# First attention fed tile group by tile group, causal quarter left constant, router chain spread between products

## Chip, cores and metric

The kernel is one Bass program on one core of a Trainium2 chip. The metric is device time in microseconds (us) of one execution. The engines are TensorE (PE in the profile, PEld for its weight loads), VectorE (DVE), ScalarE (ACT), GpSimd (POOL) and SyncE (SP), which here only issues DMAs. The cost of a wait is always seen on the engine that waits; semaphores (`then_inc`, `wait_ge`) are the only ordering between engines.

## What is computed

Two transformer blocks over x of 16 batches x 256 tokens x 128 features, fp32. The change touches the first attention and the router of the first feed-forward part:

```
x = x + attention0(layernorm(x))        # one head, width 128
    scores = triu(q @ k.T / sqrt(128)); scores = where(scores == 0, -9e15, scores)
    out = softmax(scores) @ v
h = layernorm(x)
x = x + shared(h) + routed(h)           # shared: silu(h@sg)*(h@su)@sd, width 1024
    xn = h * rsqrt(mean(h*h) + eps); logits = xn @ router_w.T   # 8 experts
    two experts a token by softmax and top_k, at most 640 tokens an expert, in order of token
x = x + attention1(layernorm(x))        # 16 heads with ALiBi bias
x = x + experts1(layernorm(x))          # one of 8 experts a token
```

`triu` keeps the keys at or behind the query's own position, so of a batch's 256 x 256 scores the block (query tile 1, key tile 0) is masked as a whole.

## The kernel before

The 4096 tokens lie as 32 tiles of 128 (`NT`), two tiles a batch (`QT = 2`, `BATCH = 16`). Each engine runs its own instruction list in order; a helper `pipelined` writes out the first and last steps of a loop and puts the middle into a hardware loop (`Fori`). The work goes through these stages.

**Statistics.** SP loads x in four chunks (`x_in`, L487), then the attention weights (L488). DVE takes bn_stats of all 32 tiles (L854), eight small operations give mean and variance of all (`norm_stats`, L839 to L846), POOL raises the variance to the power -1/2 in one instruction over 128x32 (`rsqrt`, L610), and DVE builds the 16 ALiBi tables of the second attention (L862) before it goes on.

**First attention.** One step a batch, lagged: in step b DVE normalises batch b (L870), finishes batch b-3 (reciprocal of the row sums L877, residual L881, bn_stats of the new x L886) and masks batch b-1 (scale and triangle L893, zeros to -9e15 L897, add with running minimum L901). PE in step b turns h of batch b (L1449), makes the scores of b-1 (L1457), turns the probabilities of b-2 (L1467), makes q*k and v of b (L1474, L1478) and the output of b-2 (L1489). ACT makes the exponentials of b-2 (L1229) and copies PSUM out (L1236, L1241, L1246, L1250). The copy of v(b) (L1250) waits until PE has made the output of b-2 (`pv_mm`).

**Router.** Behind the last batch come `norm_stats` again, POOL's power (L610), `r_rms` (L913 to L916) and POOL's power of that (L647). Then groups of four tiles (`GT = 4`, `NG = 8`): DVE normalises into `h4` (L924), PE turns (L1504), DVE copies (L933), ACT copies again for the shared experts (L1256), POOL copies the rows (L652), PE makes 128x8 logits (L1510). DVE then runs one chain of small dependent operations (each waits for the one ahead, `link`) from the logits to `slots_done` (L967 to L999). POOL waits for `slots_done` and sends every row to its expert with 64 indirect DMAs (L669), then builds tables (L690 to L708).

**Shared experts.** 64 products: PE writes two banks (L1531, L1532), ACT takes silu (L1266), DVE multiplies (L1011). There are two pairs of banks, so product n+2 on PE waits for DVE's product n (`hid_done`). After each group of 8 products PE makes the down product of the group before (L1554). DVE reaches its first product only when the router's chain is through.

**Later.** Routed experts (L1566 on), second attention, second expert stage. None of their code is changed.

## Time and profile before

| | |
|---|---|
| time, median of 3 executions | 962.93 us (961.61 to 963.31) |
| the profiled execution's own time, and its span | 971.0 us, 969.3 us |
| busy: PE, DVE, ACT, POOL | 80%, 54%, 42%, 45% of the span |
| chain that ended last, by engine | PE 64%, DVE 10%, issue 9%, DMA 6%, POOL 5%, ACT 2% |
| mean granted TensorE clock | 0.892 of full |

Start times are us from the span's start. The profiled execution is 0.8% longer than the median, so stretches of the trace are compared with one another, and a difference is carried over to the median. Idle time in square brackets stands ahead of an instruction and names what ended it.

### The profile page before, as it was taken

Reading aid. Unit: us, or ns where it says so; the run is one execution under the profiler, and the core shown is the slowest. Engines: PE = TensorE matmul, PEld = TensorE weight load, DVE = VectorE, ACT = ScalarE, POOL = GpSimd, SP = SyncE. Lnnn points to the kernel's source line nnn. Section 1 sums busy time; section 2 is a strip of 40 time slices with the busy share of each in tenths; the row PEclk is TensorE's granted clock in tenths of the full one; section 3 lists DMA queues with packets and bytes.
Section 4 is the critical chain, followed back from the end, with each engine's and each line's share of the span. In section 5 each row is a group of like instructions: output and inputs, shape, how many; then the busy total and the mean of one; then the engine's idle time right before and its main releaser. Section 6 shows DMA issues by size and latency. Waiting matters only on the chain.

```text
span 969.3 us, 18351 instructions
## 1 busy us (share of the span) xinstructions
PE 771.3 (80%) x5227; PEld 530.3 (55%) x5227; DVE 524.0 (54%) x2112; ACT 409.7 (42%) x1012; POOL 440.9 (45%) x770
## 2 busy tenths in 40 slices
PE   0789397999999999992279999999999981039893
PEld 0577373556555677762234556566665550038883
DVE  4688474222233232333086889899887714027672
ACT  0455121111222222321115777877877760025562
POOL 5000516777730024324425675766764432735452
PEclk9999658999999999996555999999999995569997
DMA  9970000111100032311564454554553033111110
GB/s 247 154 233 0 1 1 27 39 44 44 50 0 0 15 106 74 113 52 58 113 126 81 105 113 94 116 108 100 113 98 69 3 111 99 54 55 54 52 49 12
DMA packets 74921, 72.34 MB, mean 75 GB/s; under 512 B 8061, under 2 KB 65488, under 8 KB 72540
## 3 DMA queue, kind: packets, MB, share of 16 engines
q1 hardware_dynamic: 68428, 59.92, 28.1%
q0 software_dynamic: 5600, 11.12, 3.5%
q8 instruction: 34, 0.56, 0.3%
q10 hardware_dynamic: 816, 0.39, 0.2%
q14 instruction: 43, 0.35, 0.1%
HBM read 43.65 MB, written 27.33 MB: 73 GB/s over the span
## 4 chain that ended last, share of the span: by engine, by line
PE 64%; DVE 10%; issue 9%; DMA 6%; POOL 5%; ACT 2%; DVEq 2%; SPq 2%; POOLq 0%; ACTq 0%
PE bank L1531 10%; PE bank L1532 9%; PE bank L1677 6%; PE bank L1630 6%; PE bank L1554 6%; PE bank L1658 5%; PE bank L1583 4%; POOL sorted_rows L802 3%; DMA arena<-arena 3%; DVE rt L1082 2%; PE bank L1489 2%; PE bank L1661 2%; PE bank L1689 2%; SPq L566 1%; DVEq L1193 1%
## 5 line engine op out<-in xcount | busy, mean ns | idle before, releaser
L1082 DVE CUSTOM_DVE_ANT_0 rt<-bank,alibi 128x256 f32<-128x256 f32 x512 | 193.2, 421 | 48.3 <-PE bank L1630 41.2
L1011 DVE TENSOR_TENSOR arena<-arena,bank 128x512 f32<-128x512 f32 (+1 forms) x128 | 75.0, 587 | 194.2 <-ACT arena L1266 174.6
L1293 ACT ACTIVATE arena<-bank 128x512 f32<-128x512 f32 x256 | 151.8, 596 | 44.9 <-PE bank L1658 19.5
L1266 ACT ACTIVATE arena<-bank 128x512 f32<-128x512 f32 (+1 forms) x128 | 66.0, 517 | 209.6 <-PE bank L1532 188.5
L1531 PE MATMUL bank<-arena 128*128 128x320 f32 (+2 forms) x256 | 117.1, 539 | 10.8 <-DVE arena L1011 9.2
L1630 PE MATMUL bank<-arena 72*128 72x256 bf16 x512 | 107.6, 295 | 17.0 <-DMA arena<-qk_parts 9.6
L1532 PE MATMUL bank<-arena 128*128 128x320 f32 (+2 forms) x256 | 111.9, 519 | 0.0
L1658 PE MATMUL bank<-arena 81*128 81x256 bf16 x512 | 106.3, 281 | 5.9 <-DMA arena<-arena 4.0
L785 POOL TENSOR_TENSOR arena<-arena 128x234 f32<-128x234 f32 (+2 forms) x192 | 84.1, 473 | 28.5 <-ACT arena L1293 28.3
L1677 PE MATMUL bank<-arena 128*32 128x256 f32 x1024 | 82.7, 397 | 0.1
L1630 PEld LDWEIGHTS bank<-arena 72*128 72x128 bf16 x512 | 39.6, 103 | 76.3 <-DVE arena L1082 32.2
L722 POOL DMA_INDIRECT back_rows<-arena,back_row x40 | 39.0, 975 | 81.1 <-DVE arena L1037 71.3
L1531 PEld LDWEIGHTS bank<-arena 128*128 128x128 f32 x256 | 42.9, 193 | 58.3 <-DVE arena L1011 39.1
L669 POOL DMA_INDIRECT xg_rows<-arena,send_slot x64 | 61.9, 967 | 23.8 <-issue 13.7
L1532 PEld LDWEIGHTS bank<-arena 128*128 128x128 f32 x256 | 49.3, 193 | 42.4 <-issue 32.1
L808 POOL DMA_INDIRECT out_x<-arena,token x39 | 45.3, 1161 | 56.8 <-DVE arena L1208 50.0
L1554 PEld LDWEIGHTS bank<-arena 128*128 128x128 f32 x512 | 58.5, 192 | 6.8 <-issue 4.5
L1658 PEld LDWEIGHTS bank<-arena 81*128 81x128 bf16 x512 | 49.9, 101 | 22.3 <-DMA arena<-arena 6.4
L1764 PE MATMUL bank<-ident,arena 128*128 128x128 f32 x39 | 13.0, 333 | 61.1 <-DVE arena L1198 58.3
L1554 PE MATMUL bank<-arena 128*128 128x128 f32 x512 | 59.0, 275 | 2.3 <-DVE arena L1011 1.4
L1426 ACT ACTIVATE arena<-bank,arena 128x128 f32<-128x128 f32 x156 | 44.6, 368 | 24.3 <-PE bank L1772 24.0
L610 POOL TENSOR_TENSOR rstd<-var,minus_half 128x32 f32<-128x32 f32 x2 | 10.9, 5452 | 92.2 <-DVE var L846 92.2
(250 smaller groups left out, 1385.1 us busy)
## 6 DMA issues: line engine op xcount, KB each, us to landing
arena<-qk_parts SPq DMA_DIRECT2D x64, 192.0 KB
qk_parts<-arena SPq DMA_DIRECT2D x16, 384.0 KB, 2.8
back_rows<-empty_row SPq DMA_DIRECT2D x1, 4096.0 KB, 39.6
arena<-back_rows SPq DMA_DIRECT2D x16, 256.0 KB, 2.8
arena<-qk_parts SPq DMA_DIRECT2D x32, 128.0 KB
arena<-in_w SPq DMA_DIRECT2D x2, 2048.0 KB, 11.2
xg_rows<-empty_row SPq DMA_DIRECT2D x1, 2580.0 KB, 38.7
arena<-xg_rows SPq DMA_DIRECT2D x8, 322.5 KB, 3.9
```

Of the source, the lines that this page charges most:

```text
L669: nc.gpsimd.indirect_dma_start(out=xg_dram, out_offset=bass.IndirectOffsetOnAxis(ap=send_slot[:, k, j:j + 1], axis=0), in_=send_rows[:, k, ...
L785: last = nc.gpsimd.tensor_tensor(pr, pr, factor[:, h - FULL, first - P * k:SEQ - P * k], ALU.mult)
L1011: nc.vector.tensor_tensor(out, sil[:, k, 0:out.shape[1]], bank[4 + k][:, 0:out.shape[1]], ALU.mult).then_inc(hid_done, 1)
L1082: last = nc.vector.tensor_tensor_reduce(biased[n % 2 * QT + u], bank[n % 2][:, SEQ * u:SEQ * u + SEQ], alibi[:, h, P * (1 - u):P * (1 - u) ...
L1266: nc.scalar.activation(sil[:, k, 0:width], bank[2 + k][:, 0:width], ACT.Silu).then_inc(sil_done, 1)
L1293: nc.scalar.activation(prT3[:, n % PR].rearrange("p k t -> p (k t)"), bank[2 + n % 2][:], ACT.Exp).then_inc(exp3_done, 1)
L1531: nc.tensor.matmul(bank[2 + k][:, 0:width], wg, rhs, start=True, stop=True)
L1532: nc.tensor.matmul(bank[4 + k][:, 0:width], wu, rhs, start=True, stop=True).then_inc(gu_mm, 1)
L1554: last = nc.tensor.matmul(bank[6 + q][:, D * j:D * j + D], hidden[:, q, f, P * j:P * j + P], w_sd[:, f, :], start=(f == 0), stop=(f == 7))
L1630: last = nc.tensor.matmul(bank[n % 2][:, SEQ * u:SEQ * u + SEQ], qs[0:KROWS, c % RING, h, P * u:P * u + P], ks[0:KROWS, c % RING, h, :], s ...
L1658: last = nc.tensor.matmul(out, ks[0:KALL, c % RING, h, P * k:P * k + P], qs[0:KALL, c % RING, h, :], start=True, stop=not biases)
L1677: last = nc.tensor.matmul(bank[4][TILE * j:TILE * j + TILE, 0:SEQ], v3[:, c % VRING, u, HG * k + j, :], prT3[:, (HG * g + j) % PR, u, :], ...
```

## The change

- SP loads the attention weights ahead of x.
- The first statistics go by parts of four tiles (`part_stats`: bn_stats, then bn_aggr into `mean_var`); part 0 stands ahead of the attention, part 1 behind DVE's step 0, parts 2 and 3 behind step 1, 4 and 5 behind step 2, 6 and 7 behind step 3. POOL adds eps and takes the power for four tiles at a time.
- POOL, not DVE, makes the first normalisation of each batch (`normalise1`).
- The two query tiles' scores change places in the bank, so that the masked quarter lies at columns 0 to 127; it is set once to 9e15 in both score buffers, and DVE's mask operations work on 384 columns, not 512, PE's second score product on 128 columns, not 256.
- The second statistics are aggregated every second batch within the attention; `norm4` writes straight to `xf`, its first three groups between the last steps. DVE's copy `xf_tile` and POOL's copy of the rows go; ACT copies `xfT` from the bank, and PE makes the logits from `xfT`.
- The router's chain is cut into pieces that stand behind DVE's products 0 to 10 (`between_products`), the ALiBi tables behind products 16 to 31. PE's `count` stands behind product 5, not 1, and ACT's exponential of the router behind silu 6.

The functions `highest`, `first_of`, `totals_upto` and `ranks` hold the operations of the former `first_max` and `ranks`; `route_logits`, `route_first`, `route_second`, `route_weights`, `route_rank`, `route_slots` and `gate_norms` hold the former chain in its former order, but for `totals_upto` and `ranks`, which now stand ahead of the weights.

```diff
+PART_TILES = 4
+STATS_PARTS = NT // PART_TILES
...
+        sp.dma_start(wqkv[:], t["L0_attn_W"]).then_inc(w_in, 16)
         for c in range(XC):
             n = NT // XC
             sp.dma_start(x[:, n * c:n * c + n, :], x_dram[:, n * c:n * c + n, :]).then_inc(x_in[c], 16)
-        sp.dma_start(wqkv[:], t["L0_attn_W"]).then_inc(w_in, 16)
...
-        nc.gpsimd.affine_select(out=keep[:], in_=keep[:], compare_op=ALU.is_ge, fill=0.0, base=0,
-                                pattern=[[-P, QT], [1, SEQ]], channel_multiplier=-1).then_inc(const_done, 1)
+        nc.gpsimd.affine_select(out=keep[:], in_=keep[:], compare_op=ALU.is_ge, fill=0.0, base=-P,
+                                pattern=[[P, QT], [1, SEQ]], channel_multiplier=-1).then_inc(const_done, 1)
...
+            lo = PART_TILES * (n % STATS_PARTS)
+            r4 = rstd[:, lo:lo + PART_TILES]
             pool.wait_ge(var_done, n + 1)
-            nc.gpsimd.tensor_tensor(rstd[:], var[:], minus_half[:], ALU.pow).then_inc(rstd_done, 1)
+            nc.gpsimd.tensor_scalar(r4, mean_var[:, lo:lo + PART_TILES, 1], LN_EPS, None, ALU.add).then_inc(eps_done, 1)
+            pool.wait_ge(eps_done, n + 1)
+            nc.gpsimd.tensor_tensor(r4, r4, minus_half[:, 0:PART_TILES], ALU.pow).then_inc(rstd_done, 1)
...
-        rsqrt(0)
+        def normalise1(b):
+            if b >= 2:
+                pool.wait_ge(tr_done, b - 1)
+            pool.wait_ge(rstd_done, QT * b // PART_TILES + 1)
+            for u in range(QT):
+                i = QT * b + u
+                last = nc.gpsimd.tensor_scalar(h[:, b % 2, u, :], x[:, i, :], mean_var[:, i, 0:1], rstd[:, i:i + 1],
+                                               ALU.subtract, ALU.mult)
+            last.then_inc(ln_done, 1)
+        for b in range(BATCH):
+            for n in range(STATS_PARTS):
+                if b == (0 if n == 0 else n // 2 + 2):
+                    rsqrt(n)
+            normalise1(b)
+            if b >= 6 and b % 2 == 0:
+                rsqrt(STATS_PARTS + b // 2 - 3)
...
-        rsqrt(1)
+        for n in range(2 * STATS_PARTS - 3, 2 * STATS_PARTS):
+            rsqrt(n)
...
-        for c in range(XC):
-            n = NT // XC
-            dve.wait_ge(x_in[c], 16)
-            with dve.Fori(n // 4 * c, n // 4 * (c + 1)) as i:
-                for u in range(4):
-                    last = nc.vector.bn_stats(stats[:, 4 * i + u, :], x[:, 4 * i + u, :])
-                last.then_inc(stats_done, 1)
-        dve.wait_ge(stats_done, NT // 4)
-        norm_stats()
-        dve.wait_ge(rstd_done, 1)
-        dve.wait_ge(const_done, 2)
-        dve.wait_ge(alibi_done, 1)
-        for i in reversed(range(NH)):
-            last = nc.vector.tensor_scalar(alibi[:, i, :], alibi[:, 0, :], SLOPES[i], MAX_BIAS, ALU.mult, ALU.min)
+        def part_stats(k):
+            dve.wait_ge(x_in[k * PART_TILES // (NT // XC)], 16)
+            tiles = range(PART_TILES * k, PART_TILES * k + PART_TILES)
+            for i in tiles:
+                last = nc.vector.bn_stats(stats[:, i, :], x[:, i, :])
+            last.then_inc(parts_read, 1)
+            dve.wait_ge(parts_read, k + 1)
+            for i in tiles:
+                last = nc.vector.bn_aggr(mean_var[:, i, :], stats[:, i, :])
+            last.then_inc(var_done, 1)
+        for q in range(2):
+            nc.vector.memset(scores[:, q, 0, 0:P], -NEG)
...
+                if c % 2 == 1:
+                    dve.wait_ge(stats_done, QT * (c + 1))
+                    dve.wait_ge(var_done, STATS_PARTS + c // 2)
+                    for i in range(QT * (c - 1), QT * (c + 1)):
+                        last = nc.vector.bn_aggr(mean_var[:, i, :], stats[:, i, :])
+                    last.then_inc(var_done, 1)
...
+                raw, masked = (v[:].rearrange("p u k -> p (u k)")[:, P:QT * SEQ] for v in (scores[:, q], zeros_masked))
+                nc.vector.scalar_tensor_tensor(out=raw, in0=bank[3 + q][:, P:QT * SEQ], scalar=float(D) ** -0.5,
+                                               in1=keep[:].rearrange("p u k -> p (u k)")[:, P:QT * SEQ], op0=ALU.mult,
                                                op1=ALU.mult).then_inc(s_read, 1)
                 dve.wait_ge(s_read, c + 1)
-                nc.vector.tensor_scalar(zeros_masked[:], scores[:, q], 0.0, NEG, ALU.is_equal,
-                                        ALU.mult).then_inc(mask_a, 1)
+                nc.vector.tensor_scalar(masked, raw, 0.0, NEG, ALU.is_equal, ALU.mult).then_inc(mask_a, 1)
                 wait_apart(dve, (mask_a, c + 1))
                 for u in range(QT):
-                    last = nc.vector.tensor_tensor_reduce(scores[:, q, u, :], scores[:, q, u, :], zeros_masked[:, u, :],
-                                                          -1.0, 3e38, ALU.add, ALU.min, negmax[:, q, u:u + 1])
+                    first = P * u
+                    last = nc.vector.tensor_tensor_reduce(scores[:, q, 1 - u, first:SEQ], scores[:, q, 1 - u, first:SEQ],
+                                                          zeros_masked[:, 1 - u, first:SEQ], -1.0, -NEG if u else 3e38,
+                                                          ALU.add, ALU.min, negmax[:, q, u:u + 1])
...
-        def norm4(g, p):
-            if alive(g, NG):
-                if alive(g - 2, NG):
-                    dve.wait_ge(tr4_done, g - 1)
-                    dve.wait_ge(xf_done, g - 1)
-                for j in range(GT):
-                    last = nc.vector.tensor_scalar(h4[:, p, j, :], x[:, GT * g + j, :], mean[:, bass.ds(GT * g + j, 1)],
-                                                   rstd[:, bass.ds(GT * g + j, 1)], ALU.subtract, ALU.mult)
-                last.then_inc(h4_done, 1)
-            c, q = g - 1, 1 - p
-            if alive(c, NG):
-                dve.wait_ge(tr4_done, c + 1)
-                if alive(c - 2, NG):
-                    dve.wait_ge(router_mm, c - 1)
-                    dve.wait_ge(xfT_done, c - 1)
-                nc.vector.tensor_copy(xf_tile[:, q, :], bank[q][:]).then_inc(xft_done, 1)
...
+        def norm4(g):
+            dve.wait_ge(rstd_done, STATS_PARTS + g + 1)
+            for i in range(GT * g, GT * g + GT):
+                last = nc.vector.tensor_scalar(xf[:, i, :], x[:, i, :], mean_var[:, i, 0:1],
+                                               rstd[:, i:i + 1], ALU.subtract, ALU.mult)
+            last.then_inc(h4_done, 1)
+        part_stats(0)
+        for b in range(BATCH + 3):
+            step(b, b % 2)
+            for k in range(1, STATS_PARTS):
+                if k // 2 == b:
+                    part_stats(k)
+            if b >= BATCH:
+                norm4(b - BATCH)
+        for g in range(3, NG):
+            norm4(g)
+        dve.wait_ge(rstd_done, 2 * STATS_PARTS)
+        link(nc.vector.tensor_tensor(ln_tmp[:], mean_var[:, :, 1], rstd[:], ALU.mult))
...
+        def between_products(n):
+            if n == 0:
+                route_logits()
+            if n == 1:
+                route_first()
+            if n == 2:
+                highest(rest, rs[3])
+            if n == 3:
+                route_second()
+            if n == 6:
+                totals_upto(count_mm)
+            if n == 7:
+                ranks(rank)
+                route_rank(0)
+            if n == 8:
+                route_rank(1)
+                route_weights()
+            if n == 9:
+                route_slots()
+            if n == 10:
+                gate_norms()
+                dve.wait_ge(alibi_done, 1)
+            if 16 <= n < 32:
+                h = 31 - n
+                nc.vector.tensor_scalar(alibi[:, h, :], alibi[:, 0, :], SLOPES[h], MAX_BIAS, ALU.mult, ALU.min)
...
-            act.wait_ge(xft_done, g + 1)
-            nc.scalar.activation(xfT[:, bass.ds(GT * P * g, GT * P)], xf_tile[:, p], ACT.Copy).then_inc(xfT_done, 1)
+            act.wait_ge(tr4_done, g + 1)
+            nc.scalar.activation(xfT[:, bass.ds(GT * P * g, GT * P)], bank[p][:], ACT.Copy).then_inc(xfT_done, 1)
...
+                if isinstance(g, int) and 8 * g + c == 6:
+                    act.wait_ge(d12_done, 1)
+                    nc.scalar.activation(rs[5], rs[4], ACT.Exp).then_inc(e2_done, 1)
...
+        def turn_rows(g):
+            pe.wait_ge(h4_done, g + 1)
+            if g >= 2:
+                pe.wait_ge(xfT_done, g - 1)
+            for j in range(GT):
+                last = nc.tensor.transpose(bank[g % 2][:, P * j:P * j + P], xf[:, GT * g + j, :], ident[:])
+            last.then_inc(tr4_done, 1)
+        def route(g):
+            pe.wait_ge(xfT_done, g + 1)
+            for i in range(GT * g, GT * g + GT):
+                last = nc.tensor.matmul(bank[6][:, E0 * i:E0 * i + E0], xfT[:, P * i:P * i + P], w_router, start=True, stop=True)
+            last.then_inc(router_mm, 1)
+        turn_rows(0)
+        pe.wait_ge(att_done, QT * (BATCH - 1))
+        for g in range(NG):
+            if g + 1 < NG:
+                turn_rows(g + 1)
+            route(g)
+        pe.wait_ge(att_done, QT * BATCH)
...
-                if isinstance(g, int) and g == 0 and c == 1:
+                if isinstance(g, int) and g == 0 and c == 5:
```

How the instructions stand on DVE at the program's start, before: `stats` holds bn_stats of a tile, `arena` at L870 is h of the attention. The list is from behind the last bn_stats of the 32.

```order
L839 TENSOR_TENSOR ln_tmp<-stats 128x32 [waits stats_done]
...
L846 TENSOR_SCALAR var<-ln_tmp 128x32 [waits dve_chain]
L862 TENSOR_SCALAR alibi<-alibi 128x384 [waits alibi_done,const_done,rstd_done]
L862 TENSOR_SCALAR alibi<-alibi 128x384 x15
L870 TENSOR_SCALAR arena<-xw,mean,rstd 128x128 x4
L893 SCALAR_TENSOR_TENSOR arena<-bank,arena 128x512 [waits s_mm]
L897 TENSOR_SCALAR arena<-arena 128x512 [waits s_read]
```

And DVE of the change, from its first bn_stats to the mask of batch 0 (L896 to L904) and the part behind it:

```order
L858 BN_STATS stats<-xw 128x6 [waits x_in0]
L858 BN_STATS stats<-xw 128x6 x3
L862 BN_AGGR mean_var<-stats 128x2 [waits parts_read]
L862 BN_AGGR mean_var<-stats 128x2 x3
...
L896 SCALAR_TENSOR_TENSOR arena<-bank,arena 128x384 [waits s_mm]
L900 TENSOR_SCALAR arena<-arena 128x384 [waits s_read]
L904 ISA arena<-arena 128x256 [waits mask_a]
L904 ISA arena 128x1
L904 ISA arena<-arena 128x128
L904 ISA arena 128x1
L858 BN_STATS stats<-xw 128x6 [waits x_in1]
```

The statistics have moved from one block ahead of the attention to pieces between the masks of the first batches; the tables (L862 before) and the normalisation (L870 before) have left this place. POOL of the change, from its last constant to the third batch (`arena` is h):

```order
L638 COPY xw<-token_no 128x32 [waits const_done]
L613 TENSOR_SCALAR rstd<-mean_var 128x4 [waits var_done]
L615 TENSOR_TENSOR rstd<-rstd,minus_half 128x4 [waits eps_done]
L647 TENSOR_SCALAR arena<-xw,mean_var,rstd 128x128 [waits rstd_done]
L647 TENSOR_SCALAR arena<-xw,mean_var,rstd 128x128
...
L613 TENSOR_SCALAR rstd<-mean_var 128x4 [waits var_done]
L615 TENSOR_TENSOR rstd<-rstd,minus_half 128x4 [waits eps_done]
L647 TENSOR_SCALAR arena<-xw,mean_var,rstd 128x128 [waits rstd_done,tr_done]
L647 TENSOR_SCALAR arena<-xw,mean_var,rstd 128x128
```

POOL had one power over 128x32 here and then only constants. At the start of the shared experts DVE of the change reads (L1052 is the product):

```order
L1052 TENSOR_TENSOR arena<-arena,bank 128x512 [waits sil_done]
L973 TENSOR_TENSOR rt<-bank,arena 128x256 [waits const_done,rms_done,router_mm]
L938 TENSOR_REDUCE rs<-rt 128x32 [waits dve_chain]
L939 TENSOR_TENSOR rt<-rt,rs 128x256 [waits dve_chain]
L940 SCALAR_TENSOR_TENSOR rt<-rt,iota_e 128x256 [waits dve_chain]
L1052 TENSOR_TENSOR arena<-arena,bank 128x512 [waits sil_done,dve_chain]
L943 TENSOR_REDUCE rs<-rt 128x32
L944 TENSOR_SCALAR rs<-rs 128x32 [waits dve_chain]
L945 TENSOR_TENSOR oh<-iota_e,rs 128x256 [waits dve_chain]
```

Before, the first product stood behind the whole chain (L967 to L1003), of 48 operations. ACT of the change around the router's exponential (L1316), with the silus of products 2 to 6 ahead and product 7 behind:

```order
L1309 ACTIVATE arena<-bank 128x512 [waits hid_done,gu_mm] x5
L1316 ACT_TABLE_LOAD
L1316 ACTIVATE rs<-rs 128x32 [waits d12_done]
L1309 ACT_TABLE_LOAD [waits hid_done]
L1309 ACTIVATE arena<-bank 128x512 [waits gu_mm]
```

Before, the exponential stood ahead of all silus, with one table load behind it and none ahead.

## Rows read from the trace of the kernel before

**Rows 1.** Timeline, stretch 0:41 (start, us, engine, line, operation)
```profile
5.31 1.03 DVE L854 BATCH_NORM_STATS2 stats<-xw  x4 [5.16 <-DMA xw<-in_L_attn_x]
...
16.68 5.47 POOL L610 TENSOR_TENSOR rstd<-var,minus_half 128x32 f32<-128x32 f32 x1 [10.69 <-DVE var L846]
...
22.72 4.60 DVE L862 TENSOR_SCALAR alibi<-alibi 128x384 f32<-128x384 f32 x16 [6.12 <-POOL alibi L635]
...
27.98 0.66 PE L1449 MATMUL bank<-ident,arena 128*128 128x128 f32 x2 [15.19 <-DVE arena L870]
...
33.17 0.69 DVE L893 SCALAR_TENSOR_TENSOR arena<-bank,arena 128x512 f32<-128x512 f32 x1 [4.83 <-PE bank L1457]
...
35.23 0.60 DVE L870 TENSOR_SCALAR arena<-xw,mean,rstd 128x128 f32<-128x128 f32 x2
```

**Rows 2.** Chain that ended last, stretch 50:72 (start, us, what)
```profile
52.35 1.05 PE bank L1489 x8
...
54.45 0.69 ACT arena L1229 x3
...
55.18 0.66 PE bank L1467 x4
...
56.72 1.14 PE bank L1489 x8
```

**Rows 3.** Groups by line and form, stretch 40:95 (busy us, mean ns, idle before)
```profile
L881 DVE SCALAR_TENSOR_TENSOR xw<-bank,arena,xw 128x128 f32 x24 | 7.3, 346 | 5.7 <-PE bank L1489 5.7
L870 DVE TENSOR_SCALAR arena<-xw,mean,rstd 128x128 f32 x24 | 7.2, 343 | 0.2
```

**Rows 4.** Groups of POOL by line and form, whole span
```profile
L741 POOL TENSOR_TENSOR arena<-arena,minus_half 128x2 f32<-128x2 f32 x16 | 11.6, 724 | 1.3
...
L693 POOL TENSOR_SCALAR arena<-arena 128x384 f32<-128x384 f32 x2 | 3.0, 1515 | 0.4 <-POOL arena L690 0.2 <-POOL arena L698 0.2
L701 POOL TENSOR_SCALAR arena<-arena 128x256 f32<-128x256 f32 x7 | 2.9, 407 | 1.3 <-POOL arena L702 1.1 <-POOL arena L694 0.2
```

**Rows 5.** Groups of DVE by line and form, whole span
```profile
L1071 DVE BATCH_NORM_AGGREGATE arena<-arena 128x2 f32<-128x6 f32 x32 | 3.9, 164 | 0.6 <-DVE arena L1065 0.4
...
L943 DVE TENSOR_REDUCE rs<-rt 128x32 f32<-128x256 f32 x3 | 1.3, 420 | 0.1
```

**Rows 6.** Timeline, stretch 95:176
```profile
103.02 0.61 DVE L881 SCALAR_TENSOR_TENSOR xw<-bank,arena,xw 128x128 f32<-128x128 f32 x2 [1.89 <-PE bank L1489]
...
125.44 1.71 PE L1510 MATMUL bank<-arena 128*128 128x8 f32 x8
...
127.90 1.71 PE L1510 MATMUL bank<-arena 128*128 128x8 f32 x8
...
142.66 1.28 ACT L1266 ACT_TABLE_LOAD   x1
...
149.89 0.40 POOL L663 COPY arena<-arena 128x256 f32<-128x256 f32 x1 [13.78 <-DVE slot L999]
...
151.00 2.07 PE L1531 MATMUL bank<-arena 128*128 128x512 f32 x2 [7.44 <-DVE arena L1011]
```

**Rows 7.** Windows: start:end, us, busy of PE, PEld, DVE, ACT, POOL, clock, DMA
```profile
104.00:108.00 4.00, 0.00 (x0) 0.00 (x0) 1.40 (x9) 0.00 (x0) 2.30 (x1) 0.56 0.00 0
129.00:133.00 4.00, 4.00 (x21) 4.00 (x21) 1.70 (x5) 1.26 (x2) 0.62 (x1) 0.50 0.00 0
156.00:158.00 2.00, 2.00 (x6) 0.94 (x5) 0.45 (x2) 0.60 (x1) 1.62 (x2) 1.00 0.20 66
```

**Rows 8.** Timeline of PE, stretch 150:166
```profile
158.56 1.02 PE L1531 MATMUL bank<-arena 128*128 128x512 f32 x2
...
160.28 1.02 PE L1531 MATMUL bank<-arena 128*128 128x512 f32 x2
```

**Rows 9.** Timeline, stretch 245:345
```profile
253.68 0.96 POOL L669 DMA_INDIRECT xg_rows<-arena,send_slot x1 [0.30 <-issue]
```

**Rows 10.** Timeline, stretch 293:345
```profile
317.63 7.41 PE L1554 MATMUL bank<-arena 128*128 128x128 f32 x64 [1.41 <-DVE arena L1011]
```

176 lines of the change are left out of this document (67 added, 109 removed).

## The prediction

> **What bounds the kernel now.** I read the timeline of the first 41 us first, then the chain inside the first attention, then the timeline around the router, and last the group views for the price of each operation. The windows gave the clock.
>
> In the first stretch nothing but preparation stands ahead of PE: DVE's statistics begin at 5.31 us when the first chunk of x has landed, POOL's power over 128x32 takes 5.47 us, the ALiBi tables take 4.60 us, and PE turns batch 0 at 27.98 us [rows 1]. In the steady attention two output products of PE (L1489) start at 52.35 and 56.72 us, and the chain between them holds only ACT and PE: output of one batch, copy of v, exponentials, turn, products, output [rows 2]. DVE isn't in this ring: in the stretch 40:95 it sat idle 5.7 us ahead of its residual, for PE [rows 3]. That spacing is 4.37 us; over the twelve batches from there to the last residual (53.4 to 103.02 [rows 2, 6]) it is 4.13 us in the mean, so I take 4.3 us a batch. So a lighter DVE step alone gives nothing in the steady part; what counts is when the ring starts and when it ends.
>
> Behind it stands the hole that matters more. DVE's last residual starts at 103.02 us and ends at 103.63; I call that T0. PE gets going on the products of the shared experts for good only at 151.00, after a wait of 7.44 us for DVE's product, with two products already made [rows 6]. That is T0 + 47.4 us, and it holds the statistics, two powers over 128x32 in a row (5.47 us each by [rows 1]), router groups of 2.46 us each (125.44 to 127.90), and the router's chain. From 151.00 PE runs through to the end of the last down product at 325.04 us [rows 6, 10], at 1.72 us a product (158.56 to 160.28) [rows 8].
>
> **Part 1: the start.** Gone from the path are the 32 bn_stats but 4, the eight small operations, most of the power and the tables. The new path:
> - The attention weights are issued first; they are less than half a chunk, so I put the first chunk at 6.0 us instead of 5.31 [rows 1].
> - Four bn_stats 1.03 us [rows 1], a wait of its own on DVE 0.2 and four bn_aggr of 0.164 us that overlap [rows 5], together 0.4: 7.65 us.
> - POOL: eps 0.25, and the power over four columns. 128x2 took 0.724 us [rows 4], 128x32 5.47 us [rows 1], so 0.158 us a column and 1.04 us for four; with the hand-overs 9.05 us.
> - POOL's normalisation of 128x128 with two pointer scalars has no row. Below: the multiply-and-add over 256 columns, 0.407 us, halved with its fixed part kept, 0.25 us. Above: the dearest form, 1.515 us over 384 columns, a third of it with a fixed part, 0.6 us [rows 4]. I take 0.45 us, nearer the upper one because a pointer form is rather the dear sort; two of them give batch 0 at 10.05 us.
>
> So PE turns batch 0 at 10.1, not 27.98 us: 17.9 us earlier. Not all of it stays. The seven other parts (1.7 us each: 1.03 + 0.2 + 0.4 + hand-over) now lie between DVE's masks. A mask group took 2.06 us (33.17 to the next normalisation at 35.23, its first operation 0.69 of it [rows 1]); on three quarters of the columns I put 1.75 us (the first operation down to 0.53, the others alike). DVE's list from batch 0's scores (10.1 + 5.2 us, as 27.98 to 33.17 before [rows 1]): mask 0 15.3 to 17.05, parts 2 and 3 to 20.45, mask 1 to 22.3, parts 4 and 5 to 25.7, finish of batch 0 (reciprocal, residual, bn_stats) 1.3 and mask 2 to 28.8, parts 6 and 7 to 32.2, finish of batch 1 with four bn_aggr 1.9 and mask 3 to 35.9. Then come the two exponentials, 1.15 us (the row's 0.69 is their latter part, the rest my estimate), and 2.7 us from their end at 55.14 to the output's end at 57.86 [rows 2]: 39.8 us. Before, output 3 was the group at 52.35 with 1.05 us, so it ended at 53.4 [rows 2]. **Gain of the start: 13.6 us.** DVE, not the ring, sets the pace of the first four batches; from batch 4 on its step is 3.5 us (4.1 without the normalisation of 0.6 [rows 1] and 0.3 of mask, plus 0.3 of bn_aggr), under the ring's 4.3, and stays out of it. POOL has 0.9 + 0.65 us of work a batch against 4.3. What is queued behind its waits for `tr_done` are only its own powers and, behind batch 15, the constants that SP's `slope_set` waits for; the expert weights behind that wait are needed some 200 us later.
>
> PE's shorter score product lies in the time in which PE waits for the exponentials, so it is worth nothing.
>
> **Part 2: from T0 to the shared experts.** Groups 0 and 1 are normalised before T0, so PE turns them at once. Group 2 stands on DVE behind the last finish and its aggregates: T0 + 2.6 us; after that DVE delivers a group every 1.2 us (four of 0.343 [rows 3], which overlap a little). PE needs 2.46 us a group as long as it is at the lower of the two clock levels (1.2 of 2.4 GHz), as it was through the whole router before [rows 6, 7]. That clock had fallen to 0.56 in the mean within 104:108, right after PE stopped [rows 7]. After the change PE doesn't stop so long, but it does little there, and I expect the lower level from about T0 + 4 us on, since before a stretch of turns and 8-column products with PE busy 4.00 of 4.00 us stayed at 0.50 [rows 7]. So: T0 + 2.7 + 6 x 2.46 + last logits 1.7 = T0 + 19, less 1 us for the first groups at full rate, plus 1.4 us for the two small gate products: products start at T0 + 19.5. `rms_done` (POOL's power over 32 columns, 5.4 us, from about T0 + 9.3) comes at T0 + 14.9 and is hidden behind the router groups.
>
> **Part 3: within the shared experts.** Before, 62 products and 8 down products took 325.04 - 151.00 = 174.0 us, a climb of the clock included (at 1.00 again in 156:158 [rows 7]). Two products more at 1.72 make 177.5. Now the pieces: a dependent operation over 256 columns took 0.420 us [rows 5], 0.46 with its hand-over. Pieces 0 to 3 are 1.8, 2.0, 1.4 and 1.5 us. PE's product is 1.72 us, DVE's own product 0.69, so from the silu on there is 0.35 us of slack and 1.0 us of room a product. At the lower clock (3.4 us a product) all is hidden, at the full one each piece costs its excess; I put 1.5 us for pieces 1 to 3 together and 0.4 for 7. Piece 8 and 9 lie beside the first down product of 7.1 us, the tables (0.3 us each) fit the room. ACT's exponential brings two table loads, 1.28 us each [rows 6], and itself 0.23: 2.8 us, of which silu 7 starts 1.7 late and PE loses 1.3 after the slack. Together **3.2 us lost**. End: T0 + 19.5 + 177.5 + 3.2 = T0 + 200.2; before 325.04 - 103.63 = 221.4. **Gain 21.2 us.**
>
> The Trainium skill (ScalarE: Activation LUTs, "What ACT_TABLE_LOAD costs") prices a switch of table sets at 1.28 us and a drain behind it, 2.66 us in all. The row shows the 1.28 alone; no row here shows a switch in the middle of running silus. By the page the pieces would cost about 2.8 us more.
>
> The sends: `slots_done` comes behind product 9, about T0 + 45, so about 135 us against 149.9 [rows 6]. The last send started 103.8 us after that [rows 6, 9], so now at about 239, the tables on POOL follow for 23 us; the routed experts start at about 290. Hidden, as before.
>
> **The sum.** 13.6 + 21.2 = 34.8 us. Everything behind the shared experts is unchanged and hangs on them, so it carries: profiled execution 971.0 to 936, median 962.93 - 34.8 = **928.1 us**.
>
> **Rivals.**
> - *The router stays at full clock.* If PE's short stop no longer drops the clock, a group costs a turn of 0.66 and logits of about 1.05 us (eight weight loads and products, as L1489) [rows 2], 1.7 for 2.46: 7 x 0.75 = 5.3 us, and the slow start of the products, 2.2 us, goes too. 34.8 + 7.5 gives 920.6 us. For it: no stop over 1 us. Against: the router's stretch at 0.50 with PE busy throughout. The Trainium skill (TensorE: Matmul & The Clock Gate, "Part 4: PE-mode transpose") says that turns don't count as busy for the clock, which speaks for the lower level, and the stretch agrees.
> - *POOL and DVE hinder one another.* If every POOL operation of the attention (1.55 us a batch) stood in DVE's way, a DVE step would be 3.5 + 1.55 = 5.05 us, 0.75 over the ring, times 12, and 1.5 us in each of the four first steps: 15 us given back, 943 us; half of that, 935. In the trace POOL was idle during the attention, so nothing in it speaks against this. The Trainium skill (SBUF — State Buffer, "Who interferes with whom") says that a DVE instruction with two SBUF inputs and a POOL instruction that reads SBUF exclude one another for its whole length; the mask's last operations are such, most others of the step read PSUM.
> - *The change is slower.* One mechanism: POOL's normalisation becomes the attention's pace. A batch then takes 2a + 0.65 us for an operation of length a. Over 4.3 us (a over 1.8) it begins to cost, and 16 x (2a - 3.65) exceeds 34.8 from a = 2.9 us. The dearest row of POOL gives 0.6 for this size [rows 4], so this needs five times as much. At a = 3.2 us the time would be 972.
> - *Nothing comes of it*, because something else holds the routed experts: sends and tables would have to end 28 us later than I work out.
>
> **How the numbers follow.** Forecast (923 to 933) 0.55; full clock (917 to 923) 0.2; hindrance (933 to 943) 0.2; beyond 943 but faster 0.02; same 0.01; slower 0.02. The range 918 to 942 leaves out less than 2 in 10. A measurement of this kernel can tell 0.2% (1.9 us) from no change: faster 0.97, same 0.01, slower 0.02.
>
> **What would show it.** Right: PE's first turn of a batch near 10 us; output 3 ending near 40; DVE waiting for PE from batch 4 on; router groups 2.4 us apart at clock 0.5; last down product ending near 290 us, 35 before. Wrong: a first turn beyond 13 us (chunk late or POOL dear); ring wider than 4.3 us with waits for DVE's mask or POOL's h; groups 1.7 us apart; product spacing over 2 us at full clock in products 11 to 63; a wait of PE for `xg_in` between shared and routed experts.

## The result and the profile after

The changed kernel takes **923.36 us** (median of 4, 918.25 to 924.08) against 962.27 us (961.16 to 963.31) for the kernel before on the same chip: ratio 0.959, 95% interval 0.956 to 0.962, 38.9 us less. Forecast were 928.1 us and a range of 918 to 942. The profiled execution was 918.25 us (span 916.5), the fastest of the four. An execution over 1.5% longer than the fastest of its kernel is left out of a ratio, and not of a median. On two other chips the medians lay 38.4 and 35.4 us apart. How much of the near hit was luck stands in the part on the prediction.

The page of the changed kernel, busy time and clock by fortieths of the span:

```profile
PE 751.5 (82%) x5227; PEld 521.1 (57%) x5227; DVE 504.9 (55%) x2121; ACT 411.6 (45%) x1014; POOL 472.3 (52%) x824
...
PEclk9999699999999999975579999999999985579997
```

**Start.** Timeline of the start (columns as in [rows 1], which it answers):

```profile
3.45 0.66 PE L1483 MATMUL bank<-ident,arena 128*128 128x128 f32 x2 [3.45 <-DMA arena<-in_L_attn_W]
5.60 0.87 DVE L858 BATCH_NORM_STATS2 stats<-xw 128x6 f32<-128x128 f32 x4 [4.40 <-DMA xw<-in_L_attn_x]
6.51 0.38 DVE L862 BATCH_NORM_AGGREGATE mean_var<-stats 128x2 f32<-128x6 f32 x4
7.32 1.05 POOL L615 TENSOR_TENSOR rstd<-rstd,minus_half 128x4 f32<-128x4 f32 x1
8.48 3.15 POOL L647 TENSOR_SCALAR arena<-xw,mean_var,rstd 128x128 f32<-128x128 f32 x4
10.22 0.66 PE L1495 MATMUL bank<-ident,arena 128*128 128x128 f32 x2 [4.84 <-POOL arena L647]
```

PE turns batch 0 at 10.22 us, not 27.98. The four columns of the power took 1.05 us, a normalisation 0.79 us (3.15 for four). The chain that ended last, stretch 24:36, leads to output 3, the attention's output of batch 3 (L1535; it answers to [rows 2]):

```profile
24.88 0.76 DVE arena L904 x4
25.64 0.80 DVE stats L858 x4
26.46 0.39 DVE mean_var L862 x4
...
27.25 1.04 POOL rstd L615
...
28.59 1.05 POOL rstd L615
29.63 2.04 POOL arena L647 x2
...
31.72 0.44 PE bank L1495 x2
...
34.13 1.06 PE bank L1535 x8
```

A part costs DVE 0.80 + 0.39 us. In the chain POOL's powers and normalisation stand ahead of PE's turn of batch 5 (31.72), and that ahead of output 3 on PE. Output 3 ends at 35.2; before it was 53.4 [rows 2]. From there to the last output the ring takes 4.11 us a batch as before, and DVE and POOL both wait in it for PE (groups, stretch 40:84; it answers to [rows 3]):

```profile
L647 POOL TENSOR_SCALAR arena<-xw,mean_var,rstd 128x128 f32<-128x128 f32 x14 | 11.1, 799 | 12.7 <-PE bank L1495 12.7
...
L877 DVE SCALAR_TENSOR_TENSOR xw<-bank,arena,xw 128x128 f32<-128x128 f32 x22 | 6.7, 346 | 12.2 <-PE bank L1535 12.1
```

**Router.** PE in the stretch 88:106, and windows of the same (they answer to [rows 6, 7]):

```profile
91.51 1.71 PE L1556 MATMUL bank<-arena 128*128 128x8 f32 x8
...
93.96 1.71 PE L1556 MATMUL bank<-arena 128*128 128x8 f32 x8
...
103.37 2.08 PE L1582 MATMUL bank<-arena 128*128 128x512 f32 x2
```

```profile
96.00:100.00 4.00, 4.00 (x21) 4.00 (x21) 0.00 (x0) 1.36 (x3) 4.00 (x2) 0.50 0.00 0
```

T0, the end of the last residual, is 85.33 us. The groups are 2.45 us apart with the clock at 0.50 (0.53 in the mean over 88:104), and the first product of the shared experts starts at T0 + 18.0.

**Products with pieces.** ACT, DVE and PE around the exponential (timeline, stretch 116:126), and PE at the last down product, which answers to [rows 10]:

```profile
119.66 1.28 ACT L1316 ACT_TABLE_LOAD   x1
...
120.95 0.23 ACT L1316 ACTIVATE rs<-rs 128x32 f32<-128x32 f32 x1
121.20 1.28 ACT L1309 ACT_TABLE_LOAD   x1
...
122.49 1.08 ACT L1309 ACTIVATE arena<-bank 128x512 f32<-128x512 f32 x2
...
123.93 1.12 PE L1582 MATMUL bank<-arena 128*128 128x512 f32 x2 [1.48 <-DVE arena L1052]
```

```profile
270.36 7.41 PE L1605 MATMUL bank<-arena 128*128 128x128 f32 x64 [1.41 <-DVE arena L1052]
```

The eighth down product ends at 277.77, which is T0 + 192.4; before it was T0 + 221.4. From there to the end of the span it is 638.7 us here and was 644.3 us before, so this one profile is also 5.6 us shorter where nothing was changed.

### The profile page after: what moved, and what is told of

Same layout as the page of the kernel before. It is cut to its first block, busy times and chain, and to the rows that moved or that the text cites. A ratio compares the mean times of both kernels' runs of the same rounds, so it can differ in the third digit from the quotient of the medians.

```text
span 916.5 us, 18122 instructions
## 1 busy us (share of the span) xinstructions
PE 751.5 (82%) x5227; PEld 521.1 (57%) x5227; DVE 504.9 (55%) x2121; ACT 411.6 (45%) x1014; POOL 472.3 (52%) x824
## 4 chain that ended last, share of the span: by engine, by line
PE 65%; DVE 9%; issue 7%; DMA 6%; POOL 5%; ACT 3%; SPq 2%; DVEq 2%; POOLq 0%; ACTq 0%
PE bank L1582 10%; PE bank L1583 9%; PE bank L1728 7%; PE bank L1681 6%; PE bank L1605 6%; PE bank L1709 6%; PE bank L1634 4%; POOL sorted_rows L819 3%; DMA arena<-arena 2%; DVE rt L1125 2%; PE bank L1740 2%; SPq L566 2%; PE bank L1712 1%; PE bank L1535 1%; PE bank L1823 1%
## 5 line engine op out<-in xcount | busy, mean ns | idle before, releaser
L1052 DVE TENSOR_TENSOR arena<-arena,bank 128x512 f32<-128x512 f32 (+1 forms) x128 | 75.1, 586 | 184.9 <-ACT arena L1309 184.6
L1339 ACT ACTIVATE arena<-bank 128x512 f32<-128x512 f32 x256 | 151.6, 596 | 41.0 <-PE bank L1709 17.8
L1681 PE MATMUL bank<-arena 72*128 72x256 bf16 x512 | 105.1, 290 | 17.7 <-DMA arena<-qk_parts 8.9
L1582 PE MATMUL bank<-arena 128*128 128x320 f32 (+2 forms) x256 | 114.9, 530 | 2.3 <-DVE arena L1052 2.3
L1583 PE MATMUL bank<-arena 128*128 128x320 f32 (+2 forms) x256 | 110.5, 513 | 0.0
L1709 PE MATMUL bank<-arena 81*128 81x256 bf16 x512 | 104.2, 276 | 5.2 <-DMA arena<-arena 3.2
L1583 PEld LDWEIGHTS bank<-arena 128*128 128x128 f32 x256 | 48.7, 190 | 41.5 <-issue 31.2
L1709 PEld LDWEIGHTS bank<-arena 81*128 81x128 bf16 x512 | 48.9, 99 | 20.6 <-ACT arena L1339 6.0
L772 POOL CAST arena<-arena 128x512 bf16<-128x512 f32 x16 | 9.9, 621 | 81.6 <-ACT arena L1381 81.6
```

Of the source, the lines that this page charges most:

```text
L1052: nc.vector.tensor_tensor(out, sil[:, k, 0:out.shape[1]], bank[4 + k][:, 0:out.shape[1]], ALU.mult).then_inc(hid_done, 1)
L1339: nc.scalar.activation(prT3[:, n % PR].rearrange("p k t -> p (k t)"), bank[2 + n % 2][:], ACT.Exp).then_inc(exp3_done, 1)
L1582: nc.tensor.matmul(bank[2 + k][:, 0:width], wg, rhs, start=True, stop=True)
L1583: nc.tensor.matmul(bank[4 + k][:, 0:width], wu, rhs, start=True, stop=True).then_inc(gu_mm, 1)
L1681: last = nc.tensor.matmul(bank[n % 2][:, SEQ * u:SEQ * u + SEQ], qs[0:KROWS, c % RING, h, P * u:P * u + P], ks[0:KROWS, c % RING, h, :], s ...
L1709: last = nc.tensor.matmul(out, ks[0:KALL, c % RING, h, P * k:P * k + P], qs[0:KALL, c % RING, h, :], start=True, stop=not biases)
```

## The experiments

The twelve runs were made on three chips, four on each; there the kernel before took 970.3, 970.1 and 968.8 us in the median. So a time is set against the runs on the same chip, where there are some, and what an edit does is read mostly from stretches of the trace. norm_twice, wide_between, x_first_mask_whole and sends_late have one execution each, and each row below is one profile. This table has the ends that matter, each from a timeline row (start plus duration), in us of the kernel's own span:

```
                     T0     first down  end of 8th  span    spacing of the 8 down products
before               103.63   167.17    325.04      969.3   22.9  22.7  20.9  23.1  20.9  20.9  19.0
before_again         101.38   165.53    322.70      966.2   22.5  22.6  20.9  22.8  20.9  20.9  19.0
after                 85.33   125.75    277.77      916.5   20.9  20.9  20.9  20.9  20.9  20.9  19.0
after_again           85.58   126.05    288.51      931.9   20.9  25.6  24.8  22.9  20.9  20.9  19.0
after_third           87.22   128.70    286.79      931.0   20.9  23.7  (two: 43.2)  22.9  20.9  19.0
sends_late            85.69   126.14    278.16     1045.8   20.9  20.9  21.0  20.9  20.9  20.9  19.0
written_out           85.61   126.06    298.30      940.1   20.9  25.5  27.3  25.2  26.0  20.9  19.0
chain_whole           87.32   136.26    294.11      934.8   23.2  22.9  21.2  22.3  20.9  20.9  19.0
wide_between          87.25   126.18    283.82      925.1   20.9  23.7  22.8  21.2  21.7  20.9  19.0
wide_and_late_exp     85.27   122.88    279.59      921.7   20.9  22.7  22.9  20.9  21.8  20.9  19.0
norm_on_dve           90.51   129.35    293.44      948.6   20.9  25.6  24.8  24.5  20.9  20.9  19.0
norm_twice            92.62   134.10    292.17      938.1   20.9  23.7  22.8  20.9  22.3  20.9  19.0
x_first_mask_whole    91.71   133.24    290.99      931.1   20.9  23.7  22.9  21.0  21.9  20.9  19.0
pool_order            85.59   125.61    283.63      926.4   20.9  23.7  (two: 43.3)  22.7  20.9  19.0
```

From the end of the eighth down product to the end of the span it is 638.7 to 645.9 us in all rows but two: norm_on_dve with 655.2, and sends_late, where the routed experts wait for their rows. No edit but the sends' touches this stretch, so a difference of some 5 us between two totals says little by itself.

### Both kernels once more

No edit: the two kernels as they are.

> The kernel before, unchanged, for a second profile. In its first profile the down products of the shared experts (the group of 64 by PE) are 20.93 us apart except in three places, 22.90, 22.66 and 23.07 us, which adds 5.8 us between the first and the last of them, and the execution was 8.1 us above the median of the others. If those three places belong to the kernel (what I took in the base of 174.0 us), they stand there again and the own time stays near 970. If they belong to that one execution, the spacing is 20.93 throughout, and the own time comes out near 963 to 965.

> The changed kernel, unchanged, for a second profile. Its first profile was 918.25 us, some 5 us under its other executions (923.1 to 924.1). Both theories expect a timed median of 923 to 924 us. If the 5 us lie in the part that changed, a product spacing or a wait in the start or the router moves; if they lie behind it, the last down product ends near 277.8 us again, and the rest of the program takes about 644 us and not 638.7, as it did in the profile of the kernel before (644.3).

Before: 968.0 us, with the three wide spacings again, in the same places. So they belong to the kernel on these executions, and my base of 174.0 us for the shared experts holds 5.8 us of them. T0 is 2.25 us earlier than in the first profile; PE's clock was 1.00 in 36:40 here and 0.57 there. Changed kernel: 931.92 us (928.25 to 934.46), ratio 0.959 (0.955 to 0.963), the same as at first, though not the 923 to 924 us that I expected. Now it too has wide spacings, 10.4 us of them, and behind the eighth down product the two kernels take 643.4 and 643.5 us. Only the first profile of the changed kernel had none. By this pair the gain is 15.8 us up to T0 and 18.4 us from there to the eighth down product. What is late is ACT, with a silu whose product has long been made (ACT of after_again, stretch 126:235):

```profile
159.04 1.08 ACT L1309 ACTIVATE arena<-bank 128x512 f32<-128x512 f32 x2 [11.26 <-PE bank L1583]
...
185.47 1.09 ACT L1309 ACTIVATE arena<-bank 128x512 f32<-128x512 f32 x2 [12.13 <-remote]
```

PE had made that first product by about 156 us; ACT starts at 159.04 and then has two to do in a row. In a group without the stall it waits 8.27 us. PE then waits 2.69 us for DVE's product, and its clock is 0.65 in 160:164; so of the 4.6 us of this spacing some 2.7 are the wait and the rest is mostly the lower clock. The next group, 3.8 us too wide, has a wait of 3.56 us and the clock at 1.00.

### written_out and sends_late: where these stalls come from

```diff
-        pipelined(act, shared, NG, 0)
+        for g in range(NG):
+            shared(g, g % 2)
```

and the same on DVE and PE (written_out).

> The shared experts' loop over the eight groups of tiles is written out in full on DVE, ACT and PE instead of running partly in a hardware loop; nothing else differs from the changed kernel. In its second profile three groups took 25.56, 24.77 and 22.90 us instead of 20.93, in each of them ACT started a silu late by 2 to 4 us with nothing that the profile shows to wait for (remote or issue), while in its first profile none did. Theory (these stalls come with the instruction lists being fetched again where the loop turns): all spacings of the down products come out at 20.93 to 21 us, and the spread of the times shrinks, with a median 5 to 10 us lower where the changed kernel has these stalls. Rival (the stalls come from something else, such as the sends that POOL issues in the same time): spacings over 22 us still appear while the sends run, and the time is the same within the spread.

The theory falls: with no loop left the stalls are still there, 20.3 us in four groups, and the time is 933.22 us (ratio 0.958, 0.955 to 0.962), no better. The profile is of one of its longest executions (941.89 us), so that the stalls are larger than in after_again isn't shown.

```diff
         pool.wait_ge(slots_done, 1)
+        pool.wait_ge(down_mm, NG)
         pool.wait_ge(prefill, 48)
```

> POOL starts the 64 sends of rows to the experts only when PE has made all eight down products of the shared experts; the work is the same and only its place moves, so the routed experts must wait some 100 us for their rows and the whole time means nothing. What is looked at is the stretch of the shared experts without sends beside it. Theory (ACT is late at the head of a group of products because of what the sends do to the memory or to the fetching of instructions): none of the groups stalls, all spacings of the down products are 20.93 us but the last. Rival (the stalls belong to ACT's long idle time or to the code itself): spacings of 22.7 to 25.6 us stay, as in eight of the nine profiles with sends since the first one of before.

All spacings but the last are 20.9 to 21.0 us; the eighth down product ends at T0 + 192.5, where the first profile of the changed kernel had T0 + 192.4. PE over a whole group in which others stalled (windows; first sends_late, then after_again):

```profile
168.00:189.00 21.00, 21.00 (x98) 13.03 (x97) 8.12 (x17) 4.78 (x8) 0.00 (x0) 1.00 0.00 1
```

```profile
172.00:197.00 25.00, 21.44 (x98) 13.09 (x97) 8.88 (x18) 4.67 (x8) 19.09 (x35) 1.00 0.12 40
```

So without POOL's work of this time, the sends (or its copies for them), this run has no stalls. It is one profile, and the first one of the changed kernel had no stalls either, with the sends; the other twelve profiles with sends all have some. The places speak for it too: in after_again the last send starts at 235.3 us and no spacing behind 220.2 is wide; in chain_whole the sends come 11 us earlier (122.6 to 223.8) and the wide spacings with them, from the first one on; before, the last send was at 253.7 and the last wide spacing ended at 256.7. Why the first profile had none stays open, and so does how a send holds up ACT.

### chain_whole: the router's chain undivided

The calls in `between_products` up to product 10 stand in a row ahead of DVE's loop, `count` behind product 1, the exponential ahead of the silus:

```diff
+        route_logits()
+        route_first()
...
+        route_slots()
+        gate_norms()
         pipelined(dve, shared, NG, 1, 4)
```

> The router's chain stands undivided ahead of DVE's first product again, ACT's exponential ahead of all silus and PE's count behind product 1, as in the kernel before; everything else is as changed. Theory (the division is worth what the sum of the prediction gives it): the chain from the last logits to the end of the gate operations takes about 15 us on DVE and stops PE after two products, it saves the 3.7 us that the pieces cost now, and the clock is low again for some microseconds behind the stop: 9 to 13 us slower than the changed kernel, 932 to 936 us; a wait of PE of 8 to 12 us for the first products, clock down in it. Rival (the chain hides beside the climbing clock and the first products, and the gain came from the start and the router alone): under 4 us slower, no wait of PE over 4 us there.

935.25 us, ratio 0.962 (0.959 to 0.966) for 0.959 of the changed kernel beside it: 3 us slower, not the 9 to 13 of the theory, and as runs differ by that much, the total settles little. The stretch does (PE, timeline):

```profile
120.36 2.08 PE L1573 MATMUL bank<-arena 128*128 128x512 f32 x2 [8.15 <-DVE arena L1033]
```

The first down product comes 48.9 us behind T0, for 40.4 to 41.5 in the three profiles with the pieces: **dividing the chain, with the exponential and `count` moved, is worth 7.5 to 8.5 us** at this point. Most of it was hidden in this run's total by smaller stalls (157.9 us from the first down product to the end of the eighth, for 162.5 in after_again) and a shorter rest (640.7 for 643.4 us).

### norm_on_dve and norm_twice: the normalisation's engine

norm_on_dve puts the two operations of `normalise1(b)` back at the head of DVE's step b:

```diff
-                last = nc.gpsimd.tensor_scalar(h[:, b % 2, u, :], x[:, i, :], mean_var[:, i, 0:1], rstd[:, i:i + 1],
+                last = nc.vector.tensor_scalar(h[:, b % 2, u, :], x[:, i, :], mean_var[:, i, 0:1], rstd[:, i:i + 1],
```

> The first normalisation of each batch goes back from POOL to DVE, ahead of the batch's finish; POOL keeps the powers of the parts. Theory (in the steady part the ring of PE and ACT sets the pace, 4.11 us a batch, and DVE has about 1.2 us idle in it): two operations of 0.35 us, 0.7 us a batch, fit in; the spacing of the output products stays 4.1 us. In the first four batches DVE gets 2.8 us more work but h comes 0.9 us sooner after the power (0.35 for 0.80 us an operation) and no longer stands behind POOL's powers: between 2 us slower and 2 us faster in all, 921 to 926 us. Rival (DVE sets the pace of the first four batches, as the prediction says): output 3 ends 2.8 us later, about 38 for 35.2, and the time is 926 to 927. Second rival (DVE is full, moving this work off it was the change's gain in the steady part): spacing up to 4.3 us and more, 16 x 0.3 us = 5 us slower, 928.

In the steady part the theory holds: outputs are 4.09 and 4.41 us apart in turn, as with POOL. In the start neither number did. PE turns batch 0 earlier (9.02 for 10.1 us) but batch 2 at 18.68, where after_again does at 15.49 (PE, timeline of norm_on_dve):

```profile
18.68 0.69 PE L1497 MATMUL bank<-ident,arena 128*128 128x128 f32 x2 [3.59 <-DVE arena L868]
...
21.29 1.06 PE L1522 MATMUL bank<-arena 128*128 128x256 f32 x2
```

On DVE the normalisation of batch 2 stands behind mask 0 and parts 2 and 3; on POOL it didn't have to wait for them. PE stopped, its clock was then 0.50 in 20:24 (1.06 us for a pair that takes 0.60) and fell again to 0.65 in 32:36, and T0 came 4.9 us later. How much of that is the order and how much the clock behind it isn't split. The profile is of the longest execution, 950.91 us; the median of six is 936.14 us, 4.2 above the changed kernel beside it, and the ratios overlap (0.962, 0.957 to 0.966, for 0.959, 0.955 to 0.963).

norm_twice adds, ahead of the two operations, two more into a buffer that nobody reads:

```diff
+                nc.gpsimd.tensor_scalar(h_more[:, 0, b % 2, u, :], x[:, i, :], mean_var[:, i, 0:1], rstd[:, i:i + 1],
+                                        ALU.subtract, ALU.mult)
```

> POOL makes every first normalisation twice, the first copy into a buffer that nobody reads: four operations of 0.8 us a batch for two. Theory (in the steady ring POOL has 1.6 + 0.65 us of work in 4.25 us and is nowhere in the ring): with 3.2 + 0.65 = 3.9 us it still fits just so, the spacing of the output products stays 4.1 to 4.3 us, and only the first four batches get slower, by up to 1.6 us each: the last residual 4 to 7 us later than the 85.3 us of the changed kernel. Rival (POOL's operations hinder DVE for their length, the second rival of the prediction): each 0.8 us operation more lengthens the DVE step; 1.6 us a batch more on DVE's 3.5 us makes 5.1 us, 0.9 over the ring, so that the last residual comes another 10 us later. The operations of DVE beside them get dearer in the group view.

T0 is 7.0 us later, all of it up to output 3 (41.4 for 34.3 us), with PE's clock at 0.57 in 20:24 and 0.70 in 36:40, where after_again had 1.00; behind it eleven spacings are 4.22 us in the mean, for 4.23 in after_again, with 3.4 us of POOL's normalisation in each batch. DVE's operations beside it (groups, stretch 40:90 of norm_twice, then 40:85 of after_again):

```profile
L882 DVE SCALAR_TENSOR_TENSOR xw<-bank,arena,xw 128x128 f32<-128x128 f32 x24 | 7.3, 346 | 13.8 <-PE bank L1540 13.7
...
L909 DVE CUSTOM_DVE_ANT_0 arena<-arena 128x256 f32<-128x256 f32 x12 | 5.2, 435 | 2.2 <-DVE arena L905 2.2
```

```profile
L877 DVE SCALAR_TENSOR_TENSOR xw<-bank,arena,xw 128x128 f32<-128x128 f32 x23 | 7.1, 347 | 12.7 <-PE bank L1535 12.7
...
L904 DVE CUSTOM_DVE_ANT_0 arena<-arena 128x256 f32<-128x256 f32 x10 | 4.3, 425 | 1.9 <-DVE arena L900 1.9
```

346 for 347 ns and 435 for 425 ns: twice the work on POOL hardly touches DVE. It is POOL that loses time. The first copies (L648), which mostly fall beside DVE's last mask operations (L909), take 899 ns in the mean, the second ones (L652) 792 (norm_twice, groups in 40:90, then timeline):

```profile
L648 POOL TENSOR_SCALAR arena<-xw,mean_var,rstd 128x128 f32<-128x128 f32 x18 | 16.1, 899 | 0.0
L652 POOL TENSOR_SCALAR arena<-xw,mean_var,rstd 128x128 f32<-128x128 f32 x19 | 14.9, 792 | 0.0
```

```profile
45.04 1.97 POOL L648 TENSOR_SCALAR arena<-xw,mean_var,rstd 128x128 f32<-128x128 f32 x2
45.09 0.43 DVE L909 CUSTOM_DVE_ANT_0 arena<-arena 128x256 f32<-128x256 f32 x1 [0.19 <-DVE arena L905]
```

A pair beside the mask took 1.97 us, where one that stood clear of it took 1.57, and DVE's operation kept its 0.43. The Trainium skill (SBUF — State Buffer, "Who interferes with whom") says that a DVE instruction with two SBUF inputs and a POOL instruction that reads SBUF get in each other's way; the trace agrees, with POOL as the one that waits, up to 0.4 us a normalisation. Once in each profile of the changed kernel it went the other way: the mask operation at 24.88 us (first profile) took 0.54 us, and POOL's pair beside it 1.60.

### pool_order

```diff
             for n in range(STATS_PARTS):
-                if b == (0 if n == 0 else n // 2 + 2):
-                    rsqrt(n)
...
             normalise1(b)
+            if 3 <= b <= 5:
+                rsqrt(2 * b - 4)
+                rsqrt(2 * b - 3)
```

> Only the order of POOL's list in the first attention differs from the changed kernel: the normalisation of batch 3, 4 and 5 stands ahead of the powers of the parts that it doesn't need, and so does that of batch 1. Theory (in the first four batches POOL's list, not DVE's, is what PE waits for: 0.98 and 1.75 us ahead of the turns of batches 2 and 3, each with two powers of 1.3 us ahead of it): the wait of PE for h at batch 3 goes, output 3 ends 2 to 3 us earlier (about 32.5 for 35.2 us), the residual of batch 15 as much earlier (83 for 85.4), and the time falls by 2 to 3 us. Rival (the prediction's: DVE's masks and parts set the pace there): output 3 and the last residual move by less than 0.7 us.

The theory falls, though over a third of the chain in 24:36 was POOL's: PE's waits for h are gone there, batch 5 being turned at 30.84 for 31.98 in after_again, yet output 3 starts at 34.28 as in after_again, and T0 is 85.59 for 85.58. The exponentials of batch 3 wait for DVE's mask in both, and that ends at 31.7 behind the parts, 0.24 us later than in after_again (pool_order, timeline):

```profile
31.38 0.29 DVE L908 CUSTOM_DVE_ANT_0 arena<-arena 128x128 f32<-128x128 f32 x1
...
31.71 0.51 ACT L1278 ACTIVATE arena<-arena 128x256 f32<-128x256 f32 x1 [0.18 <-DVE arena L908]
```

In after_again these exponentials were through by 32.6 us and PE, late with batch 5 for POOL's h, turned them at 32.91; here DVE's mask is last and PE turns them at 32.86. So the two paths end within 0.3 us of one another, and shortening one alone gives nothing. The order had a price as well: PE stood still for 2.03 us ahead of 27.47, and its clock was 0.59 in 28:32. The time, 931.17 us (917.82 to 933.57), can't tell more.

### x_first_mask_whole

`x` is issued ahead of `wqkv`, and the mask's slices go back to all 512 columns:

```diff
-        sp.dma_start(wqkv[:], t["L0_attn_W"]).then_inc(w_in, 16)
         for c in range(XC):
...
+        sp.dma_start(wqkv[:], t["L0_attn_W"]).then_inc(w_in, 16)
...
-                    first = P * u
+                    first = 0
```

> Two small parts of the change are undone: x is loaded ahead of the attention weights again, and the mask and the second score product work on all 512 columns. They touch different places of the start and are read apart. Theory for the order of loads: DVE's first bn_stats starts 0.3 us earlier (5.3 for 5.6), but the weights land behind the four chunks of x, and PE needs them for the folded product at 3.45 us and for v at about 11: if they land by 9 us nothing is lost, if at 11 or later the first scores come 1 to 3 us late. Theory for the mask: a mask group takes 2.1 us for 1.79, about 1 us more by output 3 since DVE sets the pace there, and nothing in the steady ring (spacing 4.25 us). Rival: nothing of either shows in the last residual (85.4 us).

T0 is 6.1 us later. The larger part is the weights (timeline):

```profile
4.92 0.87 DVE L858 BATCH_NORM_STATS2 stats<-xw 128x6 f32<-128x128 f32 x4 [4.77 <-DMA xw<-in_L_attn_x]
...
10.80 0.66 PE L1480 MATMUL bank<-ident,arena 128*128 128x128 f32 x2 [10.80 <-DMA arena<-in_L_attn_W]
...
13.09 0.69 PE L1492 MATMUL bank<-ident,arena 128*128 128x128 f32 x2 [0.37 <-ACT arena L1260]
...
18.50 0.69 DVE L893 SCALAR_TENSOR_TENSOR arena<-bank,arena 128x512 f32<-128x512 f32 x1 [11.12 <-PE bank L1500]
```

They land at 10.8, not 3.45 us, h of batch 0 waits for them from about 9.4 on, and mask 0 starts at 18.50 instead of 14.56 to 14.93 in the three profiles of the changed kernel: **3.6 to 3.9 us for the order of two loads**. A mask group takes 2.04 us (18.50 to the next bn_stats at 20.54) for 1.71, which is 1.3 us up to output 3. The rest of the 6.1 us, the distance to after_again, is not split further; the clock was 0.80 and 0.77 in 24:28 and 28:32, where after_again had 1.00.

### wide_between and wide_and_late_exp

```diff
             last.then_inc(router_mm, 1)
+            nc.tensor.matmul(bank[2][:], w_sg[:, 0:P], xfT[:, GT * P * g:GT * P * (g + 1)], start=True, stop=True)
```

> One product of 128x512 that nobody reads is added on PE behind each router group, to see whether the lower clock of the router stretch is due to what PE does there (turns and 8-column products). Theory (it is): with a wide product in each group the granted clock rises to 1.00 within the eight groups; a group then takes about 1.7 us for its turns and logits and 0.86 for the extra product, 2.6 us, about what it takes now, and the first product of the shared experts starts within 2 us of where it does now (103.3). Rival (the stop of PE before the router set the clock and only time brings it back): the clock stays at 0.50, a group takes 2.45 + 1.7 = 4.15 us, and the first product starts some 13 us later.

The clock doesn't rise again within the groups, it never falls: 1.00 over 88:104, one window of it shown (wide_between):

```profile
96.00:100.00 4.00, 4.00 (x28) 3.19 (x27) 0.00 (x0) 1.19 (x2) 4.00 (x1) 1.00 0.00 0
```

A group with a product that nobody needs takes 2.19 us, without it 2.45, and the first down product comes at T0 + 38.9 for 40.4. The first product of the shared experts starts no earlier for it (T0 + 17.8, for 18.0 and 17.7), since the first groups ran at full clock in the changed kernel too, 1.30 us each; the 1.5 us come from the products behind, the first of which takes 1.82 us for 3.07. The clock held at 1.00 in both runs with the extra product and fell to 0.50 in all other profiles of the changed kernel and its versions. So the kind of PE's work set the clock here, not its stop. The Trainium skill (TensorE: Matmul & The Clock Gate, "Part 4: PE-mode transpose") says that turns don't count as busy for the clock in the same way; this pair agrees as far as it can, since the 8-column products were beside them.

The second version adds this to it, and `route_weights` with the gate weights behind product 11:

```diff
-                if isinstance(g, int) and 8 * g + c == 6:
+                if isinstance(g, int) and 8 * g + c == 9:
```

> The changed kernel with two additions: one product of 128x512 that nobody reads behind each router group on PE, which kept the granted clock at 1.00 through the router (first down product 38.9 us behind the end of the last residual, for 40.4), and ACT's exponential of the router behind silu 9 instead of 6, so that its two table loads lie beside the first down product; the weights follow on DVE behind product 11. Theory: the wait of PE for DVE of 1.48 us at product 9 goes, the first down product comes at 37.4 us behind the last residual, and the time is about 3 us under the changed kernel on the same chip. Rival (the wait moves to product 10 or to the down product of the second group, which needs the slots): only the 1.5 us of the clock are left.

> The changed kernel once more, on the same chip as the version beside it, for the comparison and for a third profile. Median between 923 and 932 us, as on the two chips before. If the stalls of ACT are the rule and the first profile the exception, two or three spacings of down products lie over 22 us again.

923.85 us (923.38 to 927.70), ratio 0.954 (0.952 to 0.957), against 933.37 us, ratio 0.963 (0.960 to 0.966), of the changed kernel beside it: **9 us faster**, three times what was expected. after_third came out a little over its expected 923 to 932 us, and has its wide spacings again. The place that was meant did what was expected, first down product at T0 + 37.6 (timeline):

```profile
121.06 1.13 PE L1584 MATMUL bank<-arena 128*128 128x512 f32 x2 [0.15 <-DVE arena L1053]
...
122.88 7.31 PE L1607 MATMUL bank<-arena 128*128 128x128 f32 x64
...
123.70 1.28 ACT L1317 ACT_TABLE_LOAD   x1
```

That is 3.9 us of the 9.3 us by which the two spans differ, and 2.8 us against the other two profiles of the changed kernel; this much is the edit's. The rest is 1.9 us ahead of T0 (the clock was 0.57 in after_third in 32:36, 1.00 here), 1.4 us in stalls and 2.1 us later; none of it is tied to the edit.

## Why the prediction was right, step by step

The two places were right, and so was the way in which each would gain; the sizes of the two terms were not, and that the sum came near (34.8 us, measured 38.9) is in part luck. Forecast were 13.6 us for the start and 21.2 for the rest up to the last down product. The second pair of profiles shows 15.8 and 18.4, the first pair 18.3 and 29.0, with another 5.6 where nothing was changed. Both terms have errors of some microseconds that work against each other, and the 4 us between forecast and median aren't tied to one cause.

- **First turn of batch 0 at 10.1:** 10.22. Two errors cancelled: the normalisation costs 0.79 us on POOL, above my upper bound of 0.6, while x landed 0.4 earlier, bn_stats took 0.87 for 1.03 and the wait of 0.2 wasn't there. A third of the dearest row wasn't a bound: that row has no pointer scalars. What these cost by themselves isn't shown.
- **A part 1.7 us, mask group 1.75:** 1.19 and 1.71. The term of the parts was too dear by 0.5 us, and six of the seven lie in the path: 3 of the 4.6 us by which output 3 came earlier than 39.8. Mask 0 started 0.7 us sooner than forecast, and the finishes of batches 0 and 1 make up most of the rest. The gain of the start was 18.2 us in the first pair and 15.8 by T0 in the second, not 13.6; the first pair owes 2.25 us to the lower clock of the kernel before in 36:40. That DVE sets the pace of the first four batches is half right: DVE's masks and POOL's normalisation end within 0.3 us of one another (pool_order), and that POOL's list would matter there wasn't in the forecast.
- **The order of the loads** I costed only at 0.7 us of lateness for x. That the weights were the next thing to wait for I missed: 3.6 to 3.9 us.
- **Ring 4.3 us a batch, DVE and POOL outside it:** right (4.11), also with POOL's work doubled (4.22 in the steady part, for 4.23). The rival of hindrance is ruled out as I priced it: POOL's operations don't lengthen the DVE step. DVE's masks lengthen POOL's operations, up to 0.4 us each; that stays out of the ring and stands once in the chain of the start (two normalisations 2.04 us at 29.63).
- **Router at the lower clock, groups 2.46 us:** right, 2.45; products at T0 + 18.0 for 19.5. I put the clock down to how little PE does there; wide_between bears it out. The rival of the full clock was worth 1.5 us for the first down product even with a useless product in each group. Its price of 1.7 us a group was too high: at full clock a group took 1.30 us (turns at 87.19 and 88.49 in the first profile).
- **Pieces, 3.2 us lost:** from 106.44 to 123.93 stand eight products, 17.5 us for 8 x 1.72 = 13.8, so 3.7. The table loads have no drain in the rows: the silu ahead ends at 119.64, load 119.66, exponential 120.95, load 121.20, silu 122.49. The 2.8 us more, an estimate from the Trainium skill's figure (ScalarE: Activation LUTs, "What ACT_TABLE_LOAD costs"), aren't there.
- **T0 + 200.2:** T0 + 192.4 without stalls, T0 + 202.9 with them (after_again). The base of 174.0 us held 5.8 us of stalls that I took for product time, and the products started 1.5 us sooner than forecast; these are 7.3 of the 7.8 us between T0 + 200.2 and T0 + 192.4. The changed kernel has stalls in all profiles but the first, of 5 to 20 us with its versions, so this error mostly cancels; that is the luck in the sum.
- **Nothing behind the shared experts changes:** 643.5 and 643.4 us in the second pair. In the first pair it was 644.3 and 638.7; why is open.

## What to carry to other kernels

Move an operation to another engine for what stands ahead of it in the list, not for its duration: in the profiles 0.8 us on POOL beat 0.3 on DVE, since it had not to wait for the masks and parts, though the timed medians (931.9 and 936.1 us) are too close to be sure of the gain. When preparation is cut into pieces, ask which table load was hidden in the wait before and stands between two products now. And take a base out of a long trace by its shortest period (20.93 us a group here), with the irregular ones priced apart.

## Hardware behaviour I had not expected

- POOL's `tensor_scalar` of 128x128 with two pointer scalars takes 0.79 to 0.80 us; DVE's takes 0.34.
- DVE's mask operations (two inputs in SBUF) kept their 0.43 us beside POOL's normalisation in norm_twice, and a pair of POOL's took 1.97 us for 1.57.
- Sends that POOL issues go with silus that ACT starts mostly 2 to 4 us late at the head of a group, 5 to 20 us in a run, though ACT issues no DMA in this stretch; in the one run without sends beside them there were none, and in one of thirteen profiles with them.
- One 128x512 product for every four turns and eight 8-column logits products kept the granted clock at 1.00 over 88:104, where it was 0.50 to 0.61 in the first profile, and the first down product came 1.5 us earlier with it.
